# Five chunks of 13, 13, 13, 13 and 12 sequences become 11, 14, 14, 14 and 11 in the Mamba stage

## The chip, the cores and the metric

The kernel runs on one core of one Trainium2 chip. The metric is the device time of one execution in microseconds (us). The engines are named as in the profile: PE is the matrix engine, PEld its weight loads, DVE the vector engine, ACT the scalar engine, POOL the GpSimd engine, SP the one that issues most DMAs.

## The reference, cut to what matters

The input is 64 sequences of audio; a front end makes 33 frames of 128 features out of each, so there are 64 x 33 = 2112 tokens. Eight layers follow, each with a residual. The first of them, `_L0_attn_ref`, is the one in question: three Mamba layers in a row, beside them one LSTM in both directions, and a linear layer that fuses the two.

```python
xz = jnp.einsum('bld,ed->ble', x, wi)             # 128 -> 2 x 256
xin, z = jnp.split(xz, 2, axis=-1)
u = _silu(cb + sum((xpad[:, k:k + Ls, :] * cw[:, k] for k in range(4))))
xdbl = jnp.einsum('blc,ec->ble', u, xpw)          # 32 for dt, 16 for B, 16 for C
dt = jax.nn.softplus(jnp.einsum('blr,cr->blc', dt_in, dw) + db)
def step(h, inp):                                 # over the 33 frames of a sequence
    dA = jnp.exp(dt_t[..., None] * A)
    h = dA * h + (dt_t * u_t)[..., None] * B_t[:, None, :]
    y = jnp.einsum('bcn,bn->bc', h, C_t)          # 256 channels, 16 states
y = (ys.transpose(1, 0, 2) + u * Dp) * _silu(z)
mo = jnp.einsum('blc,dc->bld', y, wo)
m = _layernorm(m + mo, ln_g[i], ln_b[i])          # three times
```

## The kernel before

All of the model is one program, stage after stage; a stage is a block in which each engine has its own list of instructions and waits on semaphores. Activations lie as [128 features, 2112 columns], the columns in the order of the sequences, 33 to a sequence. The stage `mamba_lstm` holds the layer in question. Everything is in float32.

*Items.* A Mamba layer is cut into five chunks of whole sequences (`SEQS`), so the three layers make 15 items, numbered 0 to 14: item `j` is chunk `j % 5` of layer `j // 5`. `item(j)` returns the layer, the first column and the number of columns n, 429 for 13 sequences and 396 for 12. Every buffer of the stage has room for `SCW` = 429 columns. Items 4, 9 and 14 are the 12-wide ones.

*What an item does.* For each of the 16 states there is one group, numbered g = 16j + k. In a group:

- ACT makes `dA` in PSUM, one Exp for each half of the 256 channels, 32 of the 33 frames of every sequence (`decay`, L894). `dA` has two buffers, so the decay of group g waits for the scan of group g-2.
- POOL makes `dBu` = `du` x B (L1126), also with two buffers.
- DVE runs the recurrence over both halves at once, 2n elements (`scan`, L1053), and multiplies the group before by C (`weigh`, L1063). The states lie in five buffers, `hst`.
- PE adds the weighed states to `py` by matmuls with the identity (`add`). A float32 matmul is two instructions in the profile, so `add` is four.

DVE's order is scan(g), weigh(g-1), scan(g+1) and so on, with its other work put in at fixed places: `gate` of the item before (`yz`, L1011) at k = 1, `soften` of the item after (L995, L998, L1003, which make `dt` and `du`) and `back` of the item two before (L1017) at k = 8, LSTM products (L1025 to L1037) at k = 1, 2, 5, 6, 9 and 10.

ACT's order is written out by hand as well. Beside the decays of item j it does, for item j+1, `delta` at k = 3, 4, 5 and `steps` at 7 and 8 (a softplus that keeps small values exact; L810 to L831); for item j+2, `project` at k = 7, 8, 10, 11, 14; and for item j-2, `back` at 0, 2, 8, 12 with `logs` at 7. At k = 7, 9 and twice at 11 it loads another table of functions. PE has `project` of item j+2 at k = 3, 5 (the convolution as four matmuls over shifted columns), 7, 8 and 11, `delta` of item j+1 at k = 0 and 1, `back` of j-1 at 12 and 15. Many of these share one PSUM bank, `side`.

*The LSTM.* It has 33 steps over all 64 sequences, and each of the first 11 items carries three of them (`PER_ITEM`, `LSTM_ITEMS`), whatever its width. A step goes from PE to ACT (`lstm_gates`, L871 and L872) to DVE (`ig`, `cz`) to ACT (`tc`) to DVE (`hr`) and back to PE. ACT does the gates at k = 2, 6 and 10.

*Ends.* Item 0 has no item before it that could cover it: its projection, `delta` and `soften` are done ahead of the first scan. After the last scan the last item's gate, layer norm (`back`) and `fuse` follow.

*B and C.* The rows of an item are stored to DRAM (`bc_rows`) and come back broadcast to 128 partitions, two states to a DMA, four buffers each (`Bs`, `Cs`), all on SP's queue.

A layer's item reads the `m` of the same columns of the layer before (`pe.wait_ge(m_done, j - NSC + 1)`).

Of the kernel before, what the change touches and what calls it, by code (L numbers as in the profile page):

```python
# [15 lines left out]
S = 33  # L16
# [393 lines left out]
    _at += _width  # L410
MWID = _at

SQ = 13
SEQS = [13, 13, 13, 13, 12]
NSC = len(SEQS)
SCW = SQ * S
NI = NL * NSC
LAST = NI - NSC
BG, NBS = 2, 4
# [10 lines left out]
def item(j):  # L430

    l, c = j // NSC, j % NSC
    return l, c * SCW, SEQS[c] * S


def by_seq(ap):
# [4 lines left out]
def mamba_lstm(nc, cst, w_dram, cw_dram, lstm_dram, xn, m, hT, norm):  # L441

    with ExitStack() as ctx:
        def sb(name, shape, dt=F32):
            return sbuf(nc, ctx, name, shape, dt)
# [9 lines left out]
        edge = sb("edge", [128, 5])  # L455
        u = sb("u", [128, 2, 2, SCW])
        sz = sb("sz", [128, 3, 2, SCW])
        dt = sb("dt", [128, 2, 2, SCW])
        du = sb("du", [128, 2, 2, SCW])
        xd = sb("xd", [DTR + 2 * DST + 1, 2, SCW])  # L460
        mag = sb("mag", [128, 2, SCW])
# [50 lines left out]
        def source(j):  # L512
            l, at, n = item(j)
            return (xn if l == 0 else m)[:, at:at + n]
# [13 lines left out]
        def _(sp):  # L528
# [9 lines left out]
            def store(j):  # L538
                l, at, n = item(j)
                sp.wait_ge(xd_done, j + 1)  # L540
                sp.dma_start(bc_rows[j % 3, :, 0:n], xd[DTR:DTR + 2 * DST, j % 2, 0:n]).then_inc(rows_stored, 16)

            def rows(j, first, k):
                l, at, n = item(j)
                return bc_rows[j % 3, first + BG * k:first + BG * k + BG, 0:n].unsqueeze(0).broadcast_to([128, BG, n])
# [3349 lines left out]
```

## Time and profile before

| | us |
|---|---|
| runs, median (lowest to highest) of 3 | 2210.42 (2202.44 to 2212.16) |
| the profiled execution's own time | 2202.75 |
| its span, first to last instruction | 2200.9 |
| first scan of the Mamba stage starts | 48.94 |
| next stage's first instruction | 844.53 |
| busy over the whole span: PE, DVE, ACT, POOL | 1873.3, 1626.5, 1327.4, 1013.3 |
| mean granted PE clock over the span | 0.930 |

Times in the profile are counted from the first instruction. A group of instructions is named by its line, engine and operation, then output and inputs by their names in the program, then shapes (partitions x elements). In brackets stands how long the engine sat idle before an instruction and which instruction of another engine ended that. The granted clock is a share of 2.4 GHz.

### The profile page before, as it was taken

The numbers are of one execution on the slowest core, as the hardware profiler recorded it, in microseconds if no ns is written. First come the engines' busy times: TensorE is split into PE (matmuls) and PEld (weight loads), VectorE is DVE, ScalarE is ACT, GpSimd is POOL, SyncE is SP. The second block draws the span as 40 slices with busy tenths as digits, with TensorE's granted clock in tenths as the row PEclk, the third lists the DMA queues.
The fourth block names the chain that finished last, engine by engine and source line by source line (L and its number), as shares of the span: only waits on it lengthen the run. The fifth ranks groups of instructions, "written<-read, shape, count | busy, mean of one in ns | idle before, by whom it ended". The sixth has DMA issues, their size and how long they took to land. (4 is left out here: it accounts for less than half of the span.)

```text
span 2200.9 us, 49437 instructions
## 1 busy us (share of the span) xinstructions
PE 1873.3 (85%) x19547; PEld 1375.3 (62%) x19547; DVE 1626.5 (74%) x2594; ACT 1327.4 (60%) x2696; POOL 1013.3 (46%) x778
## 2 busy tenths in 40 slices
PE   7888888888888678987877777798688699999999
PEld 4444444444443335445667777767676599999999
DVE  3999999999999994867653332336544588998897
ACT  5777787778877643133533334252346488888886
POOL 1777777777777780100046666400350033333333
PEclk9999999999999998997889889899798699999999
DMA  3444444444444432600057777501640321121100
GB/s 128 160 133 130 124 147 134 129 129 127 138 137 141 140 111 54 136 8 7 21 178 214 214 217 219 151 10 41 222 145 15 145 88 52 66 74 61 33 6 7
DMA packets 98037, 241.63 MB, mean 110 GB/s; under 512 B 15024, under 2 KB 48320, under 8 KB 95504
## 3 DMA queue, kind: packets, MB, share of 16 engines
q1 hardware_dynamic: 89120, 218.12, 32.5%
q0 software_dynamic: 7680, 15.74, 2.8%
q10 hardware_dynamic: 1008, 4.62, 0.6%
q8 instruction: 155, 2.54, 0.5%
q14 instruction: 74, 0.61, 0.1%
HBM read 226.25 MB, written 12.19 MB: 108 GB/s over the span
## 5 line engine op out<-in xcount | busy, mean ns | idle before, releaser
L1126 POOL TENSOR_TENSOR dBu<-du,Bs 128x858 f32<-128x858 f32 (+1 forms) x240 | 589.7, 2459 | 198.2 <-DVE hst L1053 109.4
L576 PE MATMUL py<-hst,ident 128*128 128x429 f32 (+1 forms) x960 | 402.1, 546 | 82.2 <-DVE hst L1063 81.6
L1053 DVE TENSOR_TENSOR_SCAN hst<-dA,dBu 128x858 f32<-128x858 f32 (+1 forms) x240 | 457.7, 1907 | 12.3 <-ACT dA L894 9.2
L894 ACT ACTIVATE dA<-dt,negA 128x416 f32<-128x416 f32 (+1 forms) x480 | 269.6, 596 | 147.6 <-DVE hst L1053 146.7
L576 PEld LDWEIGHTS py<-hst,ident 128*128 128x128 f32 x960 | 178.5, 197 | 271.1 <-DVE hst L1063 153.1
L3451 POOL TENSOR_TENSOR hm<-h,mw 128x264 f32<-128x264 f32 x128 | 90.0, 703 | 390.6 <-DVE h L3431 390.6
L1063 DVE TENSOR_TENSOR hst<-hst,Cs 128x858 f32<-128x858 f32 (+1 forms) x240 | 247.1, 1030 | 0.0
L3322 PE MATMUL pg<-hs,wh 128*128 128x66 f16 x6144 | 218.0, 193 | 6.6 <-issue 6.3
L3322 PE MATMUL pg<-xm,wi 128*128 128x66 f16 x6144 | 216.1, 195 | 4.2 <-issue 2.9
L2848 ACT ACTIVATE eh<-ph,wb 128x128 f32<-128x128 f32 x384 | 108.9, 371 | 172.5 <-PE ph L2721 115.6
L3322 PEld LDWEIGHTS pg<-hs,wh 128*128 128x128 f16 x6144 | 203.9, 98 | 10.6 <-issue 7.2
L3322 PEld LDWEIGHTS pg<-xm,wi 128*128 128x128 f16 x6144 | 203.4, 98 | 8.6 <-issue 3.3
L2721 PE MATMUL ph<-xT,wb 128*128 128x128 f32 x768 | 120.0, 306 | 55.9 <-DVE xT L2780 49.4
L2786 DVE COPY yo<-po 128x128 f32<-128x128 f32 x96 | 27.7, 288 | 174.9 <-PE po L2731 100.1
L3372 ACT ACTIVATE pg<-bz 128x1188 f32<-128x1188 f32 x128 | 149.1, 1165 | 6.2 <-PE pg L3317 2.2
L2721 PEld LDWEIGHTS ph<-xT,wb 128*128 128x128 f32 x768 | 106.8, 215 | 65.0 <-DVE xT L2780 56.7
L2695 POOL DMA_INDIRECT expert_rows<-yo,give x96 | 94.9, 989 | 74.8 <-DVE yo L2786 56.3
L3421 DVE TENSOR_TENSOR prod<-z 128x528 f32<-128x528 f32 x128 | 111.6, 872 | 17.0 <-ACT z L3382 16.7
L2690 POOL DMA_INDIRECT xi<-token_rows,take x96 | 93.6, 975 | 44.8 <-issue 43.9
L2731 PE MATMUL po<-wb,eh 128*128 128x128 f32 x768 | 111.1, 292 | 0.0
L2731 PEld LDWEIGHTS po<-wb,eh 128*128 128x128 f32 x768 | 103.8, 210 | 0.1
L3381 ACT ACTIVATE z<-pg,scale 128x528 f32<-128x528 f32 x128 | 88.2, 689 | 24.0 <-PE pg L3322 22.9
(567 smaller groups left out, 3417.2 us busy)
## 6 DMA issues: line engine op xcount, KB each, us to landing
wb<-sf_w SPq DMA_DIRECT2D x96, 514.0 KB
Bs<-bc_rows SPq DMA_DIRECT2D x96, 429.0 KB, 4.6
Cs<-bc_rows SPq DMA_DIRECT2D x96, 429.0 KB, 3.5
mw<-route_weights SPq DMA_DIRECT2D x8, 2112.0 KB, 10.1
wb<-gf_w SPq DMA_DIRECT2D x24, 514.0 KB
Bs<-bc_rows SPq DMA_DIRECT2D x24, 396.0 KB, 5.2
Cs<-bc_rows SPq DMA_DIRECT2D x24, 396.0 KB, 4.6
mb<-route_masks SPq DMA_DIRECT2D x8, 1088.0 KB, 12.6
```

What stands on the lines that cost most here:

```text
L576: return nc.tensor.matmul(out, weight, moving, **kw)
L894: last = a(o, by_seq(dt[:, j % 2, h, 0:n])[:, :, 1:S], ACT.Exp, scale=negA[:, l, h * DST + k:h * DST + k + 1])
L1053: v.tensor_tensor_scan(hst[:, g % HR, 0:2 * n], dA[:, g % 2, 0:2 * n], dBu[:, g % 2, 0:2 * n], 0.0, ALU.mult, ALU.add).then_inc(h_ready, 1)
L1063: v.tensor_tensor(h, h, Cs[:, q % NBS, k % BG, 0:n].unsqueeze(1).broadcast_to([128, 2, n]), ALU.mult).then_inc(weighed, 1)
L1126: g_.tensor_tensor(dBu[:, g % 2, 0:2 * n].rearrange("p (a n) -> p a n", a=2), du[:, j % 2, :, 0:n], Bs[:, q % NBS, k % BG, 0:n].unsqueeze( ...
L2695: pool.indirect_dma_start(ys, bass.IndirectOffsetOnAxis(ap=give[:, d:d + 1], axis=0), yo[:, d % UN, :], None).then_inc(given[d % UN][0], 16)
L2721: last = nc.tensor.matmul(ph[:, j % 2, f * ST:(f + 1) * ST], wb[:, j % UN, f * 128:(f + 1) * 128], xT[:, j % UN, :], start=True, stop=True)
L2731: last = nc.tensor.matmul(po[:, j % 2, 0:D], eh[:, j % 3, f, :], wb[:, j % UN, F + f * D:F + (f + 1) * D], start=(f == 0), stop=(f == FC - 1))
L2848: last = nc.scalar.activation(eh[:, j % 3, f, :], ph[:, j % 2, f * ST:(f + 1) * ST], act_fn, bias=wb[:, j % UN, W1 + W2 + f:W1 + W2 + f + 1])
L3322: return nc.tensor.matmul(pg[q][:, bank, c:c + CB], (wh if u else wi)[:, wp, q * HE + e, GO[z_] * D:(GO[z_] + 1) * D], rhs, start=False, s ...
L3372: a(pg[q][:, :, 0:PERB * CB], bz[:, q, :, :], ACT.Copy).then_inc(seeded[q], 1)
L3421: link(v.tensor_tensor(prod[:, q, :, :], z[:, q, 0:2, :], z[:, q, 3:5, :], ALU.mult))
```

## The change

The five chunks of each layer get 11, 14, 14, 14 and 11 sequences. The columns at which the chunks begin, so far multiples of one width, come from a table of sums, `SEQ0`. `SCW`, the room in every buffer of the stage and the length of the rows in `bc_rows`, grows from 429 to 462 columns. The 11-wide items are then 0, 4, 5, 9, 10 and 14, of 363 columns; the other nine have 462. Nothing else is changed: the order of work on each engine, the number of instructions and the places of the LSTM steps stay.

```diff
-SQ = 13
-SEQS = [13, 13, 13, 13, 12]
+SEQS = [11, 14, 14, 14, 11]
 NSC = len(SEQS)
-SCW = SQ * S
+SCW = max(SEQS) * S
+SEQ0 = [sum(SEQS[:c]) * S for c in range(NSC)]
 NI = NL * NSC
 LAST = NI - NSC
 BG, NBS = 2, 4
@@
 def item(j):
 
     l, c = j // NSC, j % NSC
-    return l, c * SCW, SEQS[c] * S
+    return l, SEQ0[c], SEQS[c] * S
```

## Rows read from the trace of the kernel before

**Rows 1.** Windows: items 0, 3, 4, 5, 11, the tail, the later stages.

```profile
core 0: us, PE busy (x) PEld busy (x) DVE busy (x) ACT busy (x) POOL busy (x), PEclk, DMA share, GB/s
48.94:103.67 54.73, 45.70 (x180) 23.83 (x180) 49.11 (x46) 45.32 (x87) 38.70 (x17) 0.90 0.42 141
...
212.20:266.25 54.05, 47.24 (x179) 24.60 (x176) 51.63 (x50) 42.04 (x82) 40.26 (x17) 0.97 0.43 127
266.25:316.93 50.68, 43.99 (x180) 23.96 (x176) 48.27 (x50) 41.55 (x82) 36.84 (x17) 1.00 0.44 133
316.93:369.80 52.87, 45.39 (x180) 23.93 (x176) 51.62 (x51) 42.52 (x82) 40.37 (x17) 1.00 0.49 147
...
637.01:686.88 49.87, 41.91 (x104) 19.52 (x104) 49.65 (x38) 35.07 (x59) 40.41 (x17) 0.93 0.51 143
...
828.09:844.23 16.14, 13.29 (x31) 5.14 (x29) 7.52 (x10) 3.83 (x7) 0.00 (x0) 1.00 0.00 0
844.23:2200.90 1356.67, 1162.19 (x17083) 1008.70 (x17083) 852.53 (x1882) 712.54 (x1546) 416.35 (x518) 0.91 0.32 97
```

**Rows 2.** Windows: the sum over all fifteen items, 48.94 to 828.09.

```profile
sum 779.15, PE 659.04 PEld 337.09 DVE 750.92 ACT 584.64 POOL 593.30; mean PE 43.94 PEld 22.47 DVE 50.06 ACT 38.98 POOL 39.55
```

**Rows 3.** Groups by shape on DVE: busy, mean ns, idle before.

```profile
L1053 DVE TENSOR_TENSOR_SCAN hst<-dA,dBu 128x858 f32<-128x858 f32 x192 | 371.4, 1935 | 9.8 <-ACT dA L894 6.7 <-POOL dBu L1126 2.1 <-issue 0.2
L1063 DVE TENSOR_TENSOR hst<-hst,Cs 128x858 f32<-128x858 f32 x192 | 200.9, 1047 | 0.0
L1053 DVE TENSOR_TENSOR_SCAN hst<-dA,dBu 128x792 f32<-128x792 f32 x48 | 86.2, 1797 | 2.5 <-ACT dA L894 2.5
L1063 DVE TENSOR_TENSOR hst<-hst,Cs 128x792 f32<-128x792 f32 x48 | 46.2, 963 | 0.0
```

**Rows 4.** Groups by shape on ACT, one operation of the softplus.

```profile
L818 ACT ACTIVATE low<-low,edge 128x858 f32<-128x858 f32 x12 | 12.1, 1012 | 0.4
...
L818 ACT ACTIVATE low<-low,edge 128x792 f32<-128x792 f32 x3 | 2.9, 958 | 0.1
```

**Rows 5.** Timeline of DVE in item 4: start, length, instruction.

```profile
284.56 0.23 DVE L1025 SCALAR_TENSOR_TENSOR ig<-gate_ps,cz 128x64 f32<-128x64 f32 x1 [0.99 <-ACT cz L872]
...
285.10 1.79 DVE L1053 TENSOR_TENSOR_SCAN hst<-dA,dBu 128x792 f32<-128x792 f32 x1
286.81 0.96 DVE L1063 TENSOR_TENSOR hst<-hst,Cs 128x792 f32<-128x792 f32 x1
287.68 0.22 DVE L1037 SCALAR_TENSOR_TENSOR hr<-gate_ps,tc 128x64 f32<-128x64 f32 x1
...
291.06 1.81 DVE L1053 TENSOR_TENSOR_SCAN hst<-dA,dBu 128x792 f32<-128x792 f32 x1 [0.57 <-ACT dA L894]
...
306.56 1.81 DVE L1053 TENSOR_TENSOR_SCAN hst<-dA,dBu 128x792 f32<-128x792 f32 x1 [0.61 <-ACT dA L894]
```

**Rows 6.** Timeline of ACT in item 4, k = 4.

```profile
274.82 1.09 ACT L894 ACTIVATE dA<-dt,negA 128x384 f32<-128x384 f32 x2 [1.58 <-DVE hst L1053]
```

**Rows 7.** Timeline of PE behind `yz`, items 3 and 5.

```profile
219.42 2.03 PE L576 MATMUL py<-u,diag 128*128 128x429 f32 x4 [1.73 <-DVE yz L1011]
221.24 3.02 PE L576 MATMUL py<-hst,ident 128*128 128x429 f32 x4
...
324.01 1.71 PE L576 MATMUL py<-u,diag 128*128 128x429 f32 x4 [1.66 <-DVE yz L1011]
```

**Rows 8.** Windows: three microseconds of item 3.

```profile
222.00:225.00 3.00, 3.00 (x7) 1.53 (x6) 3.00 (x4) 0.87 (x4) 2.50 (x2) 0.65 0.61 178
```

**Rows 9.** Groups by shape on POOL.

```profile
L1126 POOL TENSOR_TENSOR dBu<-du,Bs 128x858 f32<-128x858 f32 x192 | 478.1, 2492 | 163.4 <-DVE hst L1053 87.9 <-DVE m L1017 51.1 <-DVE du L1003 22.0
L1126 POOL TENSOR_TENSOR dBu<-du,Bs 128x792 f32<-128x792 f32 x48 | 111.5, 2324 | 34.8 <-DVE hst L1053 21.5 <-DVE m L1017 12.8
```

**Rows 10.** Timeline of PE in the opening, projection of item 0.

```profile
28.09 2.91 PE L576 MATMUL py<-xn,wt 128*128 128x429 f32 x8
```

**Rows 11.** Timeline of DVE in item 0, third and sixth scan.

```profile
54.25 1.95 DVE L1053 TENSOR_TENSOR_SCAN hst<-dA,dBu 128x858 f32<-128x858 f32 x1 [0.58 <-ACT dA L894]
...
66.02 1.95 DVE L1053 TENSOR_TENSOR_SCAN hst<-dA,dBu 128x858 f32<-128x858 f32 x1 [2.63 <-ACT dA L894]
```

## The prediction

> **What bounds the kernel now.** I read the windows first, cut at the first scan of every item. The Mamba stage lies between the first scan at 48.94 us and the next stage at 844.23; everything behind it, 1356.67 us [rows 1], has neither chunks nor a tile of this stage in it, so I take it as unchanged. In the fifteen items DVE is busy 750.92 of 779.15 us [rows 2]. It is the bound, and what it sits idle is all that a new division can change beside the opening and the tail. The idle time is length less busy time: 5.62 us in item 0, 2.42 in item 3, 2.41 in item 4, 1.25 in item 5, 0.22 in item 11 [rows 1]; 28.2 over all fifteen [rows 2]. Nearly all of it lies in items 0 to 10, the ones that also carry three LSTM steps each: behind `LSTM_ITEMS` an item has none.
>
> Then the shapes. A scan takes 1935 ns for 13 sequences (858 elements) and 1797 for 12; a weighing (`hst` times `Cs`) 1047 and 963 [rows 3]. So a sequence costs 138 ns in a scan and, with neighbours' noise in the mean, 84 in a weighing; in the timeline of item 4 a scan starts at 285.10, the weighing of 0.96 us at 286.81 and the next instruction at 287.68, so a pair of 12 takes 2.58 us [rows 5]. 138 ns for 66 elements is 2.09 each; at half of that, as 0.96 us for 792 suggests, a sequence adds 0.07 to a weighing. I use 0.14+0.07 = 0.21 us for a sequence and pair.
>
> Then who ends DVE's idle time. In item 4, the 12-wide one, it idles at three places: 0.99 us before the LSTM product `ig`, 0.57 and 0.61 before scans, each ended by ACT [rows 5]. All three are behind lumps of ACT's work for other items. ACT is not full (41.55 us in the 50.68 of item 4 [rows 1]), but it is in order and `dA` has two buffers, so a decay can start only when the scan two before it has ended, and a lump of 3 to 4 us between two decays makes the next scan late.
>
> **The change part by part.** *DVE's work.* 64 sequences stay 64, and each item has as many instructions as before. By rows 3 the cost of a scan is a fixed part and one that goes with the columns, so the sum over a layer, 13+13+13+13+12 or 11+14+14+14+11, is the same: 0 us. That 462 or 363 columns break the straight line is not shown; nothing about 396 against 429 suggests it. The same holds for `dBu` (2492 and 2324 ns [rows 9]), ACT's operations (1012 and 958 ns [rows 4]) and the matmuls. 462 columns still fit the 512 (`BANK`) that a matmul's output has in the code. A pair of an 11-wide item is about 2.58-0.21 = 2.37 us, of a 14-wide one 3.00.
>
> *The opening.* The chain up to item 0's first decay runs through PE, ACT and DVE with nothing beside it. Two sequences fewer take 66 of 429 columns: 22 matmuls in a row on the way to the delta (20 projections, 2 of the delta), 2.91 us for 8 at 429 columns [rows 10], so 0.36 x 66/429 = 0.055 us each, 1.2 us; then on ACT seven operations on both halves at 0.11 (twice the 0.054 us between 1012 and 958 ns [rows 4]) and six on one half at 0.05, 1.1; and 0.1 for decays. That is 2.4 us earlier for the third scan, which waits for ACT (it idles 0.58 us for it [rows 11]). What ACT does there for item 1 becomes 14 wide, four activations, +0.1, within the rounding. The narrower work that DVE sheds before that scan (three products of `soften` at 0.14, two scans at 0.28, a weighing at 0.14: 1.1 us) is work of the zero sum above, so the other items carry it: net -2.4+1.1 = -1.3 us.
>
> *Item 0's stalls.* The sixth scan waits 2.63 us for its decay [rows 11], which waits for item 1's delta. That chain and ACT's later lumps for items 1 and 2 stay as long as they are, so narrow pairs that lie ahead of such a wait save nothing. From the third scan to the thirteenth ten pairs at 0.41 less 0.2 for a wider `soften` would save 3.9 us. I count two pairs as saved, 0.8, and 3.1 us as more idle (bounds: 0, if every pair is saved; 5.7, if none up to the item's end is).
>
> *The 11-wide items 4, 5, 9, 10.* Worked out from item 4 [rows 5, 6]. First place: the decay at 274.82 starts at a scan's end and `ig`, which waits for ACT's `cz`, at 284.56, 9.74 us later; without its 0.99 us of waiting DVE takes 8.75. Narrower pairs take 0.63+0.07 off DVE's side, and off ACT's only 0.15 for three decays; where the next item is 14 wide (items 5 and 10) its operations add 0.27. DVE then waits 0.99+0.70-0.15+0.27 = 1.8 us; where it is 11 wide (items 4 and 9) 0.95. Second place: two pairs less 0.42, ACT +0.05 or -0.25, so 0.57 becomes 1.0 or 0.75. Third: the lump before the scan at 306.56 is for the item after next, 14 wide in all four; 0.49 off DVE's side, none off ACT's, 0.61 becomes 1.1. With 0.24 of small gaps (2.41 less the three): 4.1 us in items 5 and 10, 3.0 in 4 and 9. Bounds: as the 12-wide item now, 2.41 each, 4.6 us less in all; or an item as long as the 12-wide one, 50.68, though its work is 44.7 (4 and 9) or 45.1 (48.27 less 16 x 0.21, and the neighbours' widths): 23.2 instead of 14.2 us in the four, 9 more.
>
> *The 14-wide ones.* Here DVE has 0.21 us more per pair, so ACT's lumps fit: the two waits before scans go, `ig`'s stays where PE is late. PE is late because of its clock. In item 3, after 1.73 us of waiting for `yz`, its next eight matmuls last 2.03 and 3.02 us [rows 7], and the granted clock is 0.65 from 222 to 225 [rows 8], a mean over stretches at 1.2 and at 2.4 GHz. In item 5, after 1.66 us of the same wait, the first four take 1.71 [rows 7], and the item shows 1.00 [rows 1]. The drop costs about 1.2 us (2.42 of idle in item 3, 1.25 in item 5 [rows 1]). I leave it in items 2, 3, 7 and 8 (2.1 us idle before a 14-wide item, 1.4 before an 11-wide one), and out of 1 and 6, which come behind an 11-wide item as item 5 now comes behind the 12-wide (0.5 and 0.7, the second with the weight building). Bounds: the drop in 1 and 6 too, +3.5; nowhere, -5.
>
> Item 11 has 0.22 us now [rows 1]; I take 0.9 for items 11 to 14 together. Items 1 to 14 then sum to 23.3 us against 28.2-5.6 = 22.6: +0.7.
>
> *The layer's seam.* Project of an item needs the m of the same columns from the layer before; these were finished an item earlier, and there are still five chunks. No wait there, 0.
>
> *DMA.* The rows of B and C are the same bytes in longer and shorter lines. DVE never waited for `Cs` (0.0 before the weighings [rows 3]). An 11-wide item calls for them every 4.74 us instead of 5.6, with four buffers ahead. 0.
>
> *The tail.* From the last scan the chain is that scan, weighing, gate, centring, variance, root, scale, fusion, one after the other in 16.14 us [rows 1]. One sequence fewer: about 0.75, of which 0.35 is DVE's and goes to the others. -0.4. The 14-wide fusion ahead of the last runs on PE while ACT works on the last root.
>
> Sum: -1.3+3.1+0.7-0.4 = +2.1 us. On the profiled execution that is 2202.75+2.1 = 2204.9 (its span 2200.9 and 1.85 around it). The median of the runs lies 7.7 us higher, 2210.42, and runs at 2202.44 and 2212.16 show that executions of one kernel scatter by 0.4%. On the median the sum is 2212.5; I put the forecast midway, 2209.
>
> **The rivals.** *ACT becomes the bound of the 11-wide items* (slower). Place: items 0, 4, 5, 9, 10. For: in item 4 ACT is busy 82% of the time and already ends every wait; in item 5 it will have some 41 us of work in 49. Against: 18% of slack, and the waits don't add up now. Price: the upper bounds, +2.6 in item 0 and +9 in the four: 2.1+11.6 = 14 us, 2221 from the midway point. It is slower by over 0.5% (11 us) once item 0 is at its bound and the four idle about 5 us each.
>
> *PE's clock falls in more items* (slower). The gap before the `yz` matmuls is DVE's gate and what stands around it; behind a 14-wide item it grows by 0.07 us, and in 14-wide items PE idles more in every pair. If the clock then fell in 1 and 6 (+3.5) and in 4, 5, 9 and 10 (+1.2 each) too, the sum is 2.1+8.3 = 10 us, 2217 midway. Against: item 5, with a gap within 0.07 us of item 3's and no fall. The Trainium skill (TensorE: Matmul & The Clock Gate, HAM oscillation) says that waits between bursts of matmuls send the clock back to the half rate, so that each burst starts slow; by that rule this case is what happens, and item 5 does not bear it out for gaps of this size.
>
> *The stalls don't grow* (slightly faster). If lumps hide as they do now (-3.1-4.6) and the clock stays up in the long items (-5 at most), the sum is -5 to -10: 2199 to 2204 from 2209. For: item 5 idles only 1.25 us with all of ACT's work in it [rows 1]. Against: all three waits of item 4 are ACT's. It would still be under 0.5% unless the scatter adds to it.
>
> *POOL falls behind* (slower). `dBu` has a larger fixed part: 168 ns for a sequence [rows 9], 2.16 us at 11 against a pair of 2.37 without LSTM. The margin goes from 0.26 to 0.21 us: it stays hidden. If it took 2.49 us in all of item 14 and of another, 0.12 x 32 = 4 us.
>
> *The change does only its opening and tail*: with equal stalls -1.7 us, 2205 midway; not to be told from the forecast.
>
> **How the numbers follow.** The forecast, with its sum between -3 and +8: 0.74. ACT as bound: 0.11. The clock: 0.05. POOL: 0.02. Stalls that don't grow, or the opening and tail alone: 0.08. A measurement here can't tell a change under about 0.5%, given the 0.4% between runs. Faster by over 0.5% takes nearly every lower bound together: 0.05. Slower by over 0.5%: most of the ACT case, half of the clock's, and something of the scatter, 0.14. Within: 0.81. The range: from the forecast 10 down (stalls that don't grow, a median in the low group) and 13 up (the ACT case's lower half, a median in the upper group): 2199 to 2222.
>
> **What would show it.** Right: first scan near 46; item lengths near 47.7 in 4 and 9, 49.2 in 5 and 10, and 55.7 to 57.3 in the 14-wide ones with LSTM, 53 without; DVE's idle time before `ig` nearly 2 us in items 5 and 10, and waits of about 1 us before two scans there; none before scans in the 14-wide ones; scans of about 1.66 and 2.07 us. Wrong: an 11-wide item of 51 us or more; scans or weighings off that line; a slow clock in items 1 and 6, or in none; any DVE wait ended by `dBu` or `Cs`.

## The result and the profile after

The changed kernel takes 2211.78 us (median of 20 runs, 2206.87 to 2219.32), the kernel before on the same occasions 2203.27. The ratio is 1.0032, interval 1.0020 to 1.0044: slower by 0.32%, 7 us with 4.4 to 9.7 as its bounds (the two medians by themselves are 8.5 us apart). That is clear of noise and under the 0.5% that was taken as the mark. The forecast's own sum was +2.1 us.

The profiled execution after is the slowest of the 20: its own time is 2219.32 us around a span of 2217.4, 16.5 more than before's. The windows, cut as in [rows 1, 2], show how much of that is the stage:

```profile
core 0: us, PE busy (x) PEld busy (x) DVE busy (x) ACT busy (x) POOL busy (x), PEclk, DMA share, GB/s
46.93:101.36 54.43, 47.05 (x180) 25.70 (x181) 43.46 (x47) 45.29 (x87) 32.93 (x17) 0.81 0.43 132
...
215.94:270.49 54.55, 48.44 (x180) 24.85 (x176) 54.31 (x50) 42.14 (x82) 42.80 (x17) 0.94 0.42 128
270.49:318.33 47.84, 43.24 (x164) 23.70 (x160) 44.97 (x51) 39.74 (x82) 34.11 (x17) 0.96 0.48 124
318.33:369.09 50.76, 46.42 (x194) 26.01 (x192) 45.43 (x50) 41.71 (x82) 34.40 (x17) 0.93 0.50 143
369.09:428.03 58.94, 53.04 (x179) 25.97 (x177) 55.92 (x51) 43.76 (x82) 45.83 (x21) 0.88 0.41 132
...
587.30:637.20 49.90, 41.71 (x166) 23.11 (x162) 45.72 (x50) 41.72 (x82) 34.38 (x17) 1.00 0.48 134
...
sum 788.44, PE 676.18 PEld 342.63 DVE 751.57 ACT 586.48 POOL 593.57; mean PE 45.08 PEld 22.84 DVE 50.10 ACT 39.10 POOL 39.57
...
835.37:851.23 15.86, 12.81 (x32) 5.18 (x30) 7.22 (x10) 3.70 (x8) 0.00 (x0) 1.00 0.00 1
851.23:2217.40 1366.17, 1170.01 (x17083) 1013.32 (x17083) 854.00 (x1881) 712.66 (x1546) 416.11 (x518) 0.90 0.31 96
```

The lines are items 0, 3, 4, 5, 6 and 10, the sum of all fifteen, the tail and the later stages. Length less DVE's busy time is its idle time: 10.97 us in item 0 (5.62 before), 2.87 in item 4 (2.41), 5.33 in item 5 (1.25), 4.18 in item 10 (1.25 before: 52.86 less 51.61), 0.24 in item 3 (2.42). Over all fifteen it is 36.9 us against 28.2. DVE's work is what it was, 751.6 against 750.9.

I measure the stage from its first instruction on ACT, the table load at 24.71 us before and 25.68 after, to the next stage's at 844.53 and 851.23: 819.8 and 825.6 us, +5.7. What follows is 1356.4 and 1366.2 us long, with the same instructions.

The groups by shape, the lines that answer to [rows 3, 4, 9]:

```profile
L1053 DVE TENSOR_TENSOR_SCAN hst<-dA,dBu 128x924 f32<-128x924 f32 x144 | 298.2, 2071 | 1.7 <-ACT dA L894 1.1 <-issue 0.6
L1063 DVE TENSOR_TENSOR hst<-hst,Cs 128x924 f32<-128x924 f32 x144 | 160.6, 1115 | 0.0
L1053 DVE TENSOR_TENSOR_SCAN hst<-dA,dBu 128x726 f32<-128x726 f32 x96 | 159.2, 1660 | 18.4 <-ACT dA L894 18.4
L1063 DVE TENSOR_TENSOR hst<-hst,Cs 128x726 f32<-128x726 f32 x96 | 86.8, 905 | 0.0
...
L818 ACT ACTIVATE low<-low,edge 128x924 f32<-128x924 f32 x9 | 9.6, 1066 | 0.3
...
L1126 POOL TENSOR_TENSOR dBu<-du,Bs 128x726 f32<-128x726 f32 x96 | 203.3, 2121 | 99.9 <-DVE hst L1053 57.9 <-DVE m L1017 24.8 <-DVE du L1003 15.9
```

Scans are on the straight line (2.07 and 1.66 us). The idle time before them is split by shape: 18.4 us before the 96 narrow ones, 1.7 before the 144 wide ones. ACT ends nearly all of it.

The timeline of DVE, only lines with a wait, first item 0 (third scan, sixth scan, `ig`), then item 5:

```profile
52.74 1.67 DVE L1053 TENSOR_TENSOR_SCAN hst<-dA,dBu 128x726 f32<-128x726 f32 x1 [1.63 <-ACT dA L894]
...
65.91 1.67 DVE L1053 TENSOR_TENSOR_SCAN hst<-dA,dBu 128x726 f32<-128x726 f32 x1 [4.71 <-ACT dA L894]
70.76 0.22 DVE L1025 SCALAR_TENSOR_TENSOR ig<-gate_ps,cz 128x64 f32<-128x64 f32 x1 [2.38 <-ACT cz L872]
...
337.26 0.23 DVE L1025 SCALAR_TENSOR_TENSOR ig<-gate_ps,cz 128x64 f32<-128x64 f32 x1 [1.83 <-ACT cz L872]
343.83 1.67 DVE L1053 TENSOR_TENSOR_SCAN hst<-dA,dBu 128x726 f32<-128x726 f32 x1 [1.04 <-ACT dA L894]
359.32 1.67 DVE L1053 TENSOR_TENSOR_SCAN hst<-dA,dBu 128x726 f32<-128x726 f32 x1 [1.07 <-ACT dA L894]
```

These three waits of item 5 are the three places of [rows 5] with the sizes that were worked out (1.8, 1.0, 1.1). A fourth wait, 1.15 us before an `ig` at 324.32, is in this profile alone; without it item 5 idles 4.18 us, like item 10. The sixth scan's wait in item 0 is 4.71 us where 2.63 stood [rows 11]. ACT and PE show why:

```profile
62.85 0.56 ACT L810 ACTIVATE mag<-side 128x462 f32<-128x462 f32 x1 [3.49 <-PE side L576]
```

```profile
56.99 2.63 PE L576 MATMUL py<-u,diag 128*128 128x363 f32 x4
59.41 2.63 PE L576 MATMUL py<-hst,ident 128*128 128x363 f32 x4
61.83 0.98 PE L576 MATMUL side<-xd,w 65*128 65x462 f32 x2
...
376.88 3.45 PE L576 MATMUL py<-u,diag 128*128 128x462 f32 x4 [2.59 <-DVE yz L1011]
```

```profile
55.00:58.00 3.00, 2.68 (x4) 1.51 (x5) 2.51 (x6) 2.97 (x8) 1.71 (x2) 0.50 0.40 139
58.00:61.00 3.00, 3.00 (x6) 1.68 (x5) 3.00 (x4) 0.75 (x3) 2.13 (x1) 0.50 0.91 230
```

ACT waits 3.49 us for item 1's second delta, which stands on PE behind eight matmuls of 363 columns that take 2.4 us per four instead of 1.3, and the granted clock is 0.50, the 1.2 GHz level, from 55 to 61. The last line of the second fence is the same fall in item 6.

### The profile page after: what moved, and what is told of

The parts are those of the page before. It is cut to its first block and busy times, and to the rows that moved or that the text cites. A ratio compares the mean times of both kernels' runs of the same rounds, so it can differ in the third digit from the quotient of the medians.

```text
span 2217.4 us, 49437 instructions
## 1 busy us (share of the span) xinstructions
PE 1897.5 (86%) x19547; PEld 1385.9 (63%) x19547; DVE 1628.0 (73%) x2594; ACT 1327.3 (60%) x2696; POOL 1012.9 (46%) x778
## 5 line engine op out<-in xcount | busy, mean ns | idle before, releaser
L1126 POOL TENSOR_TENSOR dBu<-du,Bs 128x924 f32<-128x924 f32 (+1 forms) x240 | 590.3, 2463 | 204.9 <-DVE hst L1053 118.1
L576 PE MATMUL py<-hst,ident 128*128 128x462 f32 (+1 forms) x960 | 417.6, 565 | 72.0 <-DVE hst L1063 71.4
L1053 DVE TENSOR_TENSOR_SCAN hst<-dA,dBu 128x924 f32<-128x924 f32 (+1 forms) x240 | 457.4, 1906 | 20.1 <-ACT dA L894 19.5
L894 ACT ACTIVATE dA<-dt,negA 128x448 f32<-128x448 f32 (+1 forms) x480 | 269.9, 596 | 150.1 <-DVE hst L1053 149.3
L576 PEld LDWEIGHTS py<-hst,ident 128*128 128x128 f32 x960 | 183.9, 203 | 270.2 <-DVE hst L1063 144.7
L1063 DVE TENSOR_TENSOR hst<-hst,Cs 128x924 f32<-128x924 f32 (+1 forms) x240 | 247.4, 1031 | 0.0
L3421 DVE TENSOR_TENSOR prod<-z 128x528 f32<-128x528 f32 x128 | 111.6, 872 | 18.4 <-ACT z L3382 18.1
L3381 ACT ACTIVATE z<-pg,scale 128x528 f32<-128x528 f32 x128 | 88.2, 689 | 25.1 <-PE pg L3322 23.9
```

Of the source, the lines that this page charges most:

```text
L576: return nc.tensor.matmul(out, weight, moving, **kw)
L894: last = a(o, by_seq(dt[:, j % 2, h, 0:n])[:, :, 1:S], ACT.Exp, scale=negA[:, l, h * DST + k:h * DST + k + 1])
L1053: v.tensor_tensor_scan(hst[:, g % HR, 0:2 * n], dA[:, g % 2, 0:2 * n], dBu[:, g % 2, 0:2 * n], 0.0, ALU.mult, ALU.add).then_inc(h_ready, 1)
L1063: v.tensor_tensor(h, h, Cs[:, q % NBS, k % BG, 0:n].unsqueeze(1).broadcast_to([128, 2, n]), ALU.mult).then_inc(weighed, 1)
L1126: g_.tensor_tensor(dBu[:, g % 2, 0:2 * n].rearrange("p (a n) -> p a n", a=2), du[:, j % 2, :, 0:n], Bs[:, q % NBS, k % BG, 0:n].unsqueeze( ...
L3421: link(v.tensor_tensor(prod[:, q, :, :], z[:, q, 0:2, :], z[:, q, 3:5, :], ALU.mult))
```

## The experiments

Each was run against the kernel before on the same chip; a row without a ratio was timed once only, for its profile. "Stage" and "idle" are from the one profile of each row, read as above. "Rest" is what follows the stage, to the end of the span. Chips differ in the rest (see the end), so it is compared only among chips of one kind: A where it is 1356 us and more, B where it is 1305 to 1318. The B rows come from two chips, one for room, after_again, first11 and last11, the other for the rest of them.

| kernel | chunks | stage | idle, items 0 to 14 | rest | ratio to before |
|---|---|---|---|---|---|
| before | 13 13 13 13 12 | 819.8 | 28.2 | 1356.4 A | |
| before_again | same | 816.5 | 25.1 | 1306.5 B | |
| before_third | same | 821.4 | 30.3 | 1310.9 B | |
| room | same, room for 14 | 819.9 | 28.1 | 1305.7 B | 1.0003 (0.9984 to 1.0022) |
| the change | 11 14 14 14 11 | 825.6 | 36.9 | 1366.2 A | 1.0032 (1.0020 to 1.0044) |
| after_again | same | 823.0 | 33.8 | 1310.0 B | |
| first11 | 11 14 13 13 13 | 815.8 | 26.0 | 1312.7 B | 1.0028 (1.0010 to 1.0046) |
| first11_again | same | 819.6 | 30.0 | 1314.8 B | |
| first11_b | same | 822.5 | 32.4 | 1317.3 B | 1.0020 (1.0002 to 1.0037) |
| last11 | 13 13 13 14 11 | 816.2 | 25.0 | 1313.0 B | 0.9994 (0.9981 to 1.0007) |
| wide_ends | 14 12 12 12 14 | 818.8 | 25.6 | 1313.9 B | 0.9994 (0.9975 to 1.0014) |
| gf_before | 13 13 13 13 12 | 807.4 | 17.0 | 1309.5 B | 0.9961 (0.9943 to 0.9980) |
| gf_after | 11 14 14 14 11 | 821.2 | 32.4 | 1305.0 B | 0.9989 (0.9966 to 1.0012) |
| spread_after | 11 14 14 14 11 | 813.9 | 25.6 | 1358.7 A | 0.9947 (0.9926 to 0.9968) |
| gf_spread_before | 13 13 13 13 12 | 801.6 | 12.0 | 1372.0 A | 0.9906 (0.9883 to 0.9928) |
| gf_spread_after | 11 14 14 14 11 | 814.6 | 26.1 | 1305.5 B | 0.9959 (0.9933 to 0.9984) |
| nolstm_before | 13 13 13 13 12 | 780.5 | 11.0 | 1357.5 A | |
| nolstm_after | 11 14 14 14 11 | 788.0 | 19.8 | 1363.6 A | |

**room.** The buffers' length alone.

```diff
-SCW = SQ * S
+SCW = 14 * S
...
-    return l, c * SCW, SEQS[c] * S
+    return l, c * SQ * S, SEQS[c] * S
```

> Chunks of 13, 13, 13, 13 and 12 as before; only the buffers have room for 462 columns and the rows in DRAM are that long. Width theory (all of the change is in the widths, through stalls of DVE on ACT): stage length as before, 819.8 us within 1, DVE idle in the items 28 us, ratio 1.000. Layout theory (longer rows or other addresses cost something in every item): stage near 825, scans or weighings longer than 1935 and 1047 ns.

Stage 819.9, idle 28.1, item by item as before within 0.2 us. Addresses and row lengths cost nothing that shows (the interval allows 0.2%); what the change does to the stage comes from the widths.

**after_again, before_again, before_third.** The two kernels unaltered, for the scatter of a single profile.

> The changed kernel unaltered. If PE's clock falls where the program makes it fall, the same items (0, 1, 2, 6) show a mean clock of 0.81 to 0.91 and the stage is 825.5 us within 1; if the falls come by chance, other items show them and the stage moves by one to three us.

> The kernel before, unaltered, for the scatter of the stage (819.8 and, with other room, 819.9 so far) and of what follows it (1356 us on the first chip, 1306 with other room on this one). Chance: stage within 819 to 824, the rest 1305 to 1313 like the other kernels. Fixed by the program: the rest at 1306 again, 4 to 7 us under that of the changed widths.

> The kernel before for its scatter: stage 816 to 820, the rest of the span for comparison with the other three of this set.

The stage before is 816.5 to 821.4 us (with room, four profiles, mean 819.4), after 825.6 and 823.0 (mean 824.3): +4.9. Items 4, 9 and 10 repeat to 0.02 us: they idle 2.88, 2.86 and 4.19 in after_again. Items 0, 3, 5, 6 and 7 don't. This is item 6's start on PE in after_again:

```profile
374.26 1.82 PE L576 MATMUL py<-u,diag 128*128 128x462 f32 x4 [2.58 <-DVE yz L1011]
375.92 1.71 PE L576 MATMUL py<-hst,ident 128*128 128x462 f32 x4
```

PE waited 2.58 us for `yz`, as in the change's profile (2.59), and goes on at full speed where it took 3.45 us there. Item 6 then idles 0.24 instead of 3.02. So part of the falls is chance, of some 2 to 3 us on the stage, and the clue in the first of these expectations ("the same items") did not hold. In before_third item 10 starts with a fall that the other profiles of before do not have.

**first11 and last11.** One narrow chunk each.

```diff
-SEQS = [11, 14, 14, 14, 11]
+SEQS = [11, 14, 13, 13, 13]     # first11
+SEQS = [13, 13, 13, 14, 11]     # last11
```

> Chunks of 11, 14, 13, 13, 13: narrow items 0, 5, 10 only. Width theory: item 0 idles about 11 us and items 5 and 10 four to five each as in the changed kernel, items 4 and 9 fall back to about 2; opening 2.3 us shorter; stage about 3 us above before, 823. If the narrow items at the end of a layer are the cost instead, stage at or below before, 818 to 820.

> Chunks of 13, 13, 13, 14, 11: narrow items 4, 9, 14 only. Width theory: items 4 and 9 idle about 3 us each (their successor is 13 wide, so up to 4), items 0, 5, 10 as before (5.6, 1.3, 1.3), no gain in the opening, tail 0.6 shorter; stage +1 to +2 us, 821 to 822. If the narrow first chunk is not the cost, this one shows +4 or more.

> Chunks 11, 14, 13, 13, 13 once more, unaltered. Its stage was 815.8 us in one profile, 4 us under before, while its runs were 0.28% (6 us) slower. If the stage is the same in every execution, 815 to 817, the loss lies behind the stage; if falls of PE's clock come by chance, the stage comes out at 820 or more this time.

> Chunks 11, 14, 13, 13, 13 timed again. Its stage was 815.8 and 819.6 us (before 816.5 to 819.9). If the 0.28% were chance: ratio within 0.998 to 1.0015. If something behind the stage costs, 1.002 to 1.004 again with a rest of the span 5 us or more above that of the kernel before on the same chip.

In last11 items 4 and 9 idle 3.65 and 3.58 us, as expected, but items 3 and 8, 14 wide, save more than that (0.24 and 1.27 against 2.4), and the stage is 816.2, under the 821 to 822 that were expected: no loss in its one profile, and none in the runs.

In first11 items 5 and 10 idle 4.0 in all three profiles and item 0 7.6, 7.6 and 10.8, against the 11 that were expected; the opening's gain pays for that, and the stage averages 819.3, the same as before and not the expected 823. Yet its runs are 0.20 and 0.28% slower. The rest of its span is 1312.7 us where room has 1305.7 on the same chip, and 1314.8 and 1317.3 where the three profiles of before's widths on the other chip have 1306.5 to 1310.9. So this loss seems to lie behind the stage, in stages with the same instructions. In two of the three profiles one place makes most of it. Between two table loads on ACT, around the matmuls of L2420 to L2432, before_again and then first11_again show:

```profile
1040.57:1072.39 31.82, 26.18 (x130) 16.04 (x130) 17.79 (x86) 18.59 (x33) 2.22 (x4) 0.89 0.11 28
```

```profile
1043.28:1081.61 38.33, 33.24 (x130) 20.85 (x130) 19.80 (x88) 18.80 (x33) 2.22 (x4) 0.69 0.10 25
```

Third from the end stands the mean granted clock. The same 130 matmul instructions take 6.5 us longer with a mean granted clock of 0.69 instead of 0.89. first11_b, wide_ends and gf_spread_before have this stretch as long (38.3 to 38.4 us, 0.69); the other fourteen profiles, first11's own among them, have it at 31.5 to 33.4. Whether narrow first chunks make such a fall more likely isn't shown: over the timed runs the mean granted clock is 0.936 and 0.937 in the two sets of first11 and 0.944 and 0.942 in the kernel before beside them, but wide_ends has 0.938 against 0.942 and no loss in its runs. last11 and wide_ends have rests as long as first11's (1313.0, 1313.9) and lose nothing in the runs, so a single profile's rest says little.

**wide_ends.** The change turned round: `SEQS = [14, 12, 12, 12, 14]`.

> Chunks of 14, 12, 12, 12, 14 with the order of before. Stall theory: item 0 idles 3 to 4 us (before 5.6), items 5 and 10 none before scans, 1 to 1.5 in all; the 12-wide items 1 to 3, 6 to 8 idle about 2 to 3 each as item 4 does now; opening 1.2 us longer, tail 1 longer; stage 818 to 822, so no loss like the changed kernel's in spite of the longer ends. If instead unequal chunks cost whatever their order, 824 or more.

Nearly as expected: stage 818.8, item 0 idles 2.5 (3 to 4 expected), items 5 and 10 1.6, the 12-wide items 1.1 to 3.0. Unequal chunks as such are not the loss. What the narrow items lose among wide ones has no counterpart here.

**gf_before and gf_after.** `gate` first at k = 1, on either kernel.

```diff
+                if j >= 1 and k == 1:
+                    gate(j - 1)
                 if j < LSTM_ITEMS:
                     if k in (1 if j else 2, 5, 9):
                         lstm_c(PER_ITEM * j + (k - 1) // 4)
...
-                if j >= 1 and k == 1:
-                    gate(j - 1)
```

> Chunks as before; DVE makes yz (gate) ahead of the LSTM products at k = 1 instead of behind them, so PE waits some 0.6 us less. If that gap lets PE's clock fall and the late matmuls then hold up ACT and the product ig, the items 1, 2, 3, 6, 7, 8 idle 1.2 us instead of 2.4, clock 1.00, stage 812 to 814, ratio 0.997. If the clock falls for another reason, the idle times stay and the stage is 820.

> The changed kernel with the same move of gate. If the falls are the gap's, items 1, 2, 6, 7 lose 1 to 1.5 us of idle each; those of the 11-wide items (2.9 in 4 and 9, 4.2 in 5 and 10), put down to ACT's lumps and not to the clock, stay. Stage 817 to 819. If the 11-wide items idle for PE's sake, they fall too.

The windows of gf_before, items 3 and 4 and the sum:

```profile
208.72:260.68 51.96, 47.02 (x179) 24.39 (x176) 51.45 (x50) 42.00 (x82) 40.22 (x17) 0.97 0.45 132
260.68:310.94 50.26, 45.41 (x180) 24.44 (x176) 48.28 (x51) 41.54 (x82) 36.84 (x17) 0.97 0.44 134
...
sum 766.73, PE 658.38 PEld 336.21 DVE 749.69 ACT 584.53 POOL 593.14; mean PE 43.89 PEld 22.41 DVE 49.98 ACT 38.97 POOL 39.54
```

Item 3 idles 0.51 us instead of 2.42, item 4 1.98 instead of 2.41. The stage is 12 us shorter and the runs 0.39% faster, more than expected: the 13-wide items' wait is the late start of PE behind `yz`, and the fall of its clock there. These are the eight microseconds from that start in item 3, of before and then of gf_before:

```profile
219.42:227.42 8.00, 8.00 (x31) 4.16 (x31) 8.00 (x7) 4.08 (x10) 5.45 (x4) 0.79 0.39 114
```

```profile
215.41:223.41 8.00, 8.00 (x41) 4.85 (x42) 7.97 (x10) 6.58 (x14) 5.64 (x3) 1.00 0.37 121
```

PE waits 1.21 us for `yz` instead of 1.73, and none of gf_before's items 1 to 14 starts with a fall. What a fall costs shows where one item has it in one profile of before and not in another: item 1 idles 2.37 and 1.20 us, item 2 2.71 and 1.11, item 6 1.79 and 0.49, item 10 2.86 and 1.25, so 1.2 to 1.6 us each. The prediction's 1.2 for it was near.

On the changed kernel the same move takes the wait out of items 2, 3, 6, 7 and 8 (0.24 to 0.47 each) and leaves the narrow ones: 2.6 us in 4 and 9, 10.9 in item 0. Items 5 and 10 do not stay at 4.2 as expected but idle 6.1 and 4.7: in item 5 DVE now reaches `gate` before PE has finished `py` and waits 2.36 us there. The stage, 821.2, is above the expected 817 to 819, and the runs show no difference from before.

**spread_after, gf_spread_before, gf_spread_after.** Two of ACT's operations moved: the third `low` behind the LSTM gates of k = 6, the logarithm of `e` behind the decay of k = 8.

```diff
                     a(low[:, :, 0:n], low[:, :, 0:n], ACT.Exp, scale=-1.0, bias=edge[:, 4:5]).then_inc(w_ready, 1)
+                if k == 6:
                     act.wait_ge(w_ready, j + 1)
                     a(low[:, :, 0:n], low[:, :, 0:n], ACT.Square, scale=KAPPA, bias=edge[:, 1:2]).then_inc(sq_w_ready, 1)
...
                     a(low[:, :, 0:n], low[:, :, 0:n], ACT.Ln, bias=edge[:, 2:3]).then_inc(low_logged, 1)
+                if k == 8:
                     act.wait_ge(e_ready, j + 1)
                     a(e[:, :, 0:n], e[:, :, 0:n], ACT.Ln, bias=edge[:, 0:1]).then_inc(ln_ready, 1)
-                if k == 8:
...
-                if j + 1 < NI and k in (3, 4, 5):
+                if j + 1 < NI and k in (3, 4, 5, 6):
                     delta(j + 1, k)
```

> The changed kernel with two of ACT's softplus operations a place later: the third `low` behind the LSTM gates at k = 6 instead of ahead of them at k = 5, the logarithm of `e` behind the decay at k = 8 instead of ahead of it at k = 7. Theory (ACT's lumps for a 14-wide successor come too close together for narrow pairs): the wait before ig (1.8 us in items 5 and 10, 0.8 in 4 and 9) falls by 1 us and the one before the next scan goes, so items 5 and 10 idle 2.2 to 2.6 instead of 4.2, 4 and 9 1.3 to 1.6 instead of 2.9; stage 4 to 7 us shorter than 824. Rival (the waits are PE's, through its clock, and ACT's order is no matter): idle times as in the changed kernel.

> Chunks as before, with gate ahead of the LSTM products and the two softplus operations later. Gate ahead alone left 17.1 us of idle, two thirds of it in items 0, 4 and 9. If the theory of ACT's lumps holds, items 4 and 9 fall from 2.0 to under 1.2 and item 0 by 1 to 2; stage 803 to 806, ratio 0.994 to 0.996 against before. If it doesn't, stage 807.

> The changed chunks with gate ahead and the two softplus operations later. If the loss of the change is its stalls: less of them, but item 0 and items 5 and 10 keep some (10 and 3 us), so the stage is 810 to 812, still 9 to 10 us above the 801.6 that the chunks of before have with the same two moves, ratio about 0.994 to 0.995 against before. If the stalls were only the clock's and the lumps', both gone now: 800 to 803.

The windows of spread_after, items 4 and 5 and the sum:

```profile
266.24:313.10 46.86, 42.47 (x176) 23.82 (x176) 44.84 (x51) 39.60 (x82) 34.10 (x17) 1.00 0.48 127
313.10:361.72 48.62, 42.72 (x183) 24.00 (x179) 45.53 (x51) 41.60 (x82) 34.37 (x17) 1.00 0.52 148
...
sum 776.80, PE 659.36 PEld 336.52 DVE 751.18 ACT 584.95 POOL 593.51; mean PE 43.96 PEld 22.43 DVE 50.08 ACT 39.00 POOL 39.57
```

Items 4 and 5 idle 2.02 and 3.09 us, 0.9 and 1.1 to 2.2 less than with the change alone, with as much work on every engine. The gain is smaller than was expected, by 0.5 us each. The three places of item 5 show what the moves did (this kernel is one line longer ahead of them):

```profile
329.80 0.23 DVE L1026 SCALAR_TENSOR_TENSOR ig<-gate_ps,cz 128x64 f32<-128x64 f32 x1 [0.73 <-ACT cz L873]
336.36 1.67 DVE L1054 TENSOR_TENSOR_SCAN hst<-dA,dBu 128x726 f32<-128x726 f32 x1 [1.04 <-ACT dA L895]
351.93 1.67 DVE L1054 TENSOR_TENSOR_SCAN hst<-dA,dBu 128x726 f32<-128x726 f32 x1 [1.08 <-ACT dA L895]
```

The wait before `ig` fell from 1.83 to 0.73 us; in item 4 it went from 0.84 to nothing. Both waits before scans stayed, 0.70 and 1.08 in item 4 and 1.04 and 1.08 here, though the first of them was expected to go. So the order of ACT's work is shown as the cause for the `ig` waits. For the waits before scans the trace names ACT's `dA`, but the moves left them: the last one is 1.07 or 1.08 us in items 4, 5, 9 and 10 in gf_spread_after too, and the one ahead of it shrinks there only in items 4 and 9, to 0.4. PE's clock is not the difference in item 4: its mean is 1.00 here and in after_again, with 2.02 and 2.88 us of idle time.

The stage is 10 us shorter than the changed kernel's mean, more than the expected 4 to 7. The four narrow items behind item 0 give 4.5 us of it, the six 14-wide ones with LSTM 5.3.

Both moves on the chunks of before give the fastest kernel of the study, 0.9906 of before, its stage 801.6 us. With the same two moves the changed chunks have 814.6. This is item 0 and the sum, first of gf_spread_before:

```profile
48.76:102.30 53.54, 45.17 (x180) 23.75 (x180) 49.12 (x47) 45.00 (x87) 38.71 (x17) 0.92 0.43 145
...
sum 760.90, PE 647.52 PEld 332.14 DVE 748.92 ACT 583.20 POOL 593.01; mean PE 43.17 PEld 22.14 DVE 49.93 ACT 38.88 POOL 39.53
```

then of gf_spread_after:

```profile
46.03:99.66 53.63, 45.86 (x180) 25.27 (x180) 43.46 (x46) 44.99 (x87) 32.90 (x17) 0.84 0.44 134
...
sum 777.45, PE 670.59 PEld 340.14 DVE 751.33 ACT 585.37 POOL 593.25; mean PE 44.71 PEld 22.68 DVE 50.09 ACT 39.02 POOL 39.55
```

Item 0 is as long with 11 sequences as with 13, 53.5 and 53.6 us: DVE has 5.7 us less to do in it and idles 5.8 us more. Idle time differs by 14.1 us in all (26.1 less 12.0); the other 8.4 us are those of items 5 and 10 (2.6 and 3.7 against 0.5 each) and item 14 (3.8, two waits for ACT, against 0.15), less small gains elsewhere. The stage was expected at 810 to 812. The changed chunks lose 4.9 us in the stage with the old order and 13 with the better one, where one profile stands on either side; in the runs the better order has 0.9959 against 0.9906, with intervals that do not meet, though on chips of different kinds.

**nolstm_before and nolstm_after.** All LSTM steps left out and `hs` set to zero, so the output lacks the LSTM.

```diff
-LSTM_ITEMS = S // PER_ITEM
+LSTM_ITEMS = 0
...
-                pe.wait_ge(hs_kept, S)
+                pe.wait_ge(hs_kept, 1)
...
-            lstm(0)
...
-            lstm_gates(0)
...
-            lstm_cell(0)
...
+            v.memset(hs[:, :, :], 0.0).then_inc(hs_kept, 1)
```

> Chunks as before, with all 33 LSTM steps left out and hs set to zero (its output is not the reference's). Items without LSTM steps idle 0.2 to 0.4 us now, so items 1 to 10 should too; item 0 under 3 us; stage 785 to 792.

> The changed chunks, LSTM steps left out as well. Theory (the loss is stalls that only the LSTM items have): with them gone only the gain of the opening and the tail is left and this one is 1 to 2 us shorter than nolstm_before in the stage. Rival (narrow items stall for ACT with no LSTM too, as item 14's 0.5 us hints): items 4, 5, 9, 10 idle 1 us or more each and the stage is longer than nolstm_before's by 2 us or more.

Item 5 of nolstm_before and of nolstm_after:

```profile
299.36:349.14 49.78, 41.03 (x104) 19.15 (x104) 49.56 (x38) 35.17 (x59) 40.32 (x17) 0.97 0.51 158
```

```profile
302.40:348.22 45.82, 39.14 (x104) 19.81 (x104) 43.49 (x38) 34.43 (x59) 34.36 (x17) 0.93 0.55 158
```

The rival won: with no LSTM the changed chunks are 7.5 us longer in the stage, one profile against one. Item 5 idles 0.22 us at 13 and 2.33 at 11 wide, item 0 5.4 and 10.1. Narrow items stall with no LSTM step too, but less: items 4, 5, 9 and 10 idle 1.28, 2.33, 1.28 and 2.04 us, about half of what they do with it. What goes is the wait before `ig` and the one before the scan of k = 8, which so hang on the LSTM; the last wait for `dA`, before the scan of k = 12, stays 1.07 us in items 4, 5 and 9, and item 5 has another of 1.06, ended by PE's `py`. The first expectation missed in its details: nolstm_before's stage, 780.5, is under the 785 to 792 expected, its item 0 idles 5.4 us and not under 3, and its items 4, 6 and 9 idle 0.8 to 1.1 us.

## Why the prediction was wrong, point by point

Two steps failed: the one from the sum to the time, which turned a loss into a gain, and the term for the idle time of items 1 to 14, which was too small by 2.6 us.

*The level.* The sum was made against the profiled execution, then put "midway" between two levels, which gave 2209. That is 1.4 us below the median of 2210.42 that was shown, so the number forecast a slightly faster kernel for a change whose own sum was +2.1 us. The step mixed a difference with a guess about the base. The base was in truth low, 2203.27 over 20 runs, and the changed kernel is slower clear of noise. That 2211.78 lies near 2209 is luck: the base was taken too high and the loss too small.

*DVE's work*: 0 forecast, +0.7 and +1.1 us measured over the items (751.57 and 752.02 against 750.92). Right.

*The opening*: 2.4 us forecast, the third scan comes 29.54 us after the stage's start before and 27.06 after, 2.48. Right, as was the tail in the main (16.44 to 15.86, 0.6 instead of 0.75).

*Item 0*: from its third scan to the end it was to lose 2.6 us in length (5.7 of work less, 3.1 of idle more). It lost 0.8 in the profile and 2.4 in after_again, from 49.4 (49.3 to 51.0 in the four profiles of before's widths). Right by mechanism, too small by up to 1.8 when the slow clock meets it. With the better order (gf_spread) the narrow item 0 loses only 0.4 us from its third scan on, near the stated bound.

*Items 4 and 9, 5 and 10*: 3.0 and 4.1 us forecast; 2.87 and 2.87, 5.33 and 4.18, and 4.18 and 4.19 in after_again. Right, place by place, but for the wait of 1.15 us that item 5 has in one profile. spread_after shows ACT's order as the cause of the waits before `ig`; for those before scans it is what the trace names, and the moves did not touch the last of them, so for that one ACT is argued and not tested.

*The 14-wide items*: here the largest part of the miss lies. Items 1, 2, 3, 6, 7, 8 were given 0.5, 2.1, 1.4, 0.7, 2.1, 1.4; they show 1.9, 2.2, 0.2, 3.0, 0.8, 1.3, and 1.8, 2.2, 1.3, 0.2, 2.4, 1.3 in after_again. The total was 8.2 and came out at 9.4 and 9.2; where the clock falls is partly chance, and it was treated as fixed by item. The fall was left out of items 1 and 6 because they come behind an 11-wide item, "as item 5 now comes behind the 12-wide", where the gap is 1.66 us. Their gaps are in fact the longest: PE waits 2.50 us for `yz` in item 1 (1.86 before) and 2.58 or 2.59 in item 6 (2.10 before). Item 1 started with a fall in both profiles, and in the first it waits 1.33 us for `cz`; item 6 did in one. Behind a 14-wide item the gap was to grow by 0.07 us; it grows by 0.25 to 0.4, from 1.68 to 1.96 in item 2 and from 1.73 to 1.98 and 2.11 in item 3. By the prediction's own list, a slow clock in items 1 and 6 was a sign of being wrong.

*The baseline of idle time* was one profile's 22.6 us in items 1 to 14. Four profiles of before's widths average 21.9, two of the change 25.2: +3.3 where +0.7 stood. This is the term of the sum that was mis-sized. Of the 2.6 us the 14-wide items make 1.1, the baseline 0.7, the four narrow items 0.5 and the last four 0.3. With it the sum of +2.1 becomes +4.7, and the stage measures +4.9 in the mean.

*The rivals.* ACT as the bound of the narrow items was priced at +14 and refused; the measured case lies between it and the forecast. PE's clock falls in more items: it does not. Behind `yz` it fell in six, four, six and six items of the four profiles of before's widths, and in five and six of the change's two; it moved to other items. In item 6 it fell after a gap of 2.59 us and not after one of 2.58, so the gap alone does not decide. The Trainium skill (TensorE: Matmul & The Clock Gate, Part 1: The HAM clock gate) says that the number of matmuls at the low clock varies between runs of one kernel; these two traces agree, with the same four matmul instructions of item 6 in 3.45 us and in 1.82. "The stalls don't grow" was priced wrongly in the prediction: its sums of -5 to -10 us were taken from 2209, which already holds the +2.1, so it is 2197 to 2202 and not 2199 to 2204. POOL took 2121 ns at 11 wide and held up no scan in the profile, as forecast.

*Still open*: the stage explains 4.9 of 7 us; the interval begins at 4.4, so it may be all. Whether the stages behind it add 1 to 3 us, as first11's runs hint, isn't settled. In the first profiles they are 9.8 us longer with the change, at a granted clock of 0.90 against 0.91; after_again's 1310.0 lies among those of before's widths (1305.7 to 1310.9). An opening in which PE is kept at full clock was not tried.

## What to carry to other kernels

A narrow chunk shortens the bound engine's work at once, but the work that the other engines do in its shadow belongs to its neighbours and keeps their width; so a narrow chunk between wide ones can turn hidden work into waits. Reckon idle time at each place where the bound engine waits, as the other engine's path against its own, and shift the order of that other engine's work before touching the sizes: two moved operations and one moved product gave 0.94% here, and none of the four divisions tried beat before's by itself. Take a baseline from several profiles when the terms are of 1 to 3 us.

## What the runs showed of the hardware

The granted clock falls to 0.50 and stays there for 6 us and more in item 0 of the change, with PE at work in that time (busy 2.68 and 3.00 of 3.00 us from 55 to 61). After the same gap, 2.59 and 2.58 us, it was low once and full once. A fall behind `yz` cost 1.2 to 1.6 us of DVE's time in a 13-wide item. With gaps of 0.8 to 1.8 us gf_before has no fall in fourteen item starts, where before has six in fourteen with gaps of 1.3 to 2.1. In 4 of 18 profiles a later stretch of 130 matmul instructions took 38.3 us at 0.69 instead of some 32 at 0.89.

The chips differ in one stage. It runs from 1117.03 to 1431.96 us in before's first profile and from 1115.43 to 1387.60 in before_again's, with the same instructions:

```profile
1117.03:1431.96 314.93, 244.33 (x1762) 230.15 (x1762) 112.95 (x403) 112.41 (x392) 188.50 (x192) 0.88 0.67 195
```

```profile
1115.43:1387.60 272.17, 225.39 (x1762) 210.47 (x1762) 116.31 (x403) 113.33 (x391) 188.40 (x192) 0.95 0.80 226
```

The DMAs that stream the experts' weights there moved 195 GB/s on one occasion and 226 on the other, 43 us of difference, six times the effect studied. The other profiles fall in line: 314.9 to 318.5 us in all six of kind A, 270.3 to 273.0 in all twelve of kind B. So times were compared only within one set.
